# Sine by polynomial on GpSimd, weight splits in order of use, and the first recurrence of a two-layer kernel two steps later

## What is computed

```python
nu = jax.nn.softplus(nu_log); mag = jnp.exp(-jnp.exp(nu)); theta = jnp.exp(theta_log)
A_re = mag * jnp.cos(theta);  A_im = mag * jnp.sin(theta)
gamma = jnp.sqrt(jnp.clip(1.0 - mag * mag, 0.0))
# Bu = x @ (gamma * B).T ; h_t = A * h_{t-1} + Bu_t (complex) ; 32 states
y = einsum(H_re, C_re) - einsum(H_im, C_im) + D * x
h = jax.nn.gelu(einsum('lne,he->lnh', x, proj1) + proj1_bias, approximate=False)
out = einsum('lnh,eh->lne', h, proj2) + proj2_bias
```

## Time and profile before

| | |
|---|---|
| median of the runs | 805.11 us (804.58 to 806.72) |
| the profiled execution, its own time | 806.05 us |
| its span from first to last instruction | 804.2 us |
| PE busy in the span | 783.7 us (97%) |
| DVE, ACT, POOL busy | 699.9, 524.0, 468.4 us |

### The profile page before, as it was taken

The page is one execution under the profiler, slowest core; times in us unless marked ns, Lnnn a source line. Parts: engine busy times, 40 slices in busy tenths (PEclk is TensorE's granted clock), DMA queues, the critical chain, the costliest instruction groups (busy, mean ns, idle before and its releaser), DMA issues.

```text
span 804.2 us, 23023 instructions
## 1 busy us (share of the span) xinstructions
PE 783.7 (97%) x7912; PEld 717.5 (89%) x7912; DVE 699.9 (87%) x2647; ACT 524.0 (65%) x1612; POOL 468.4 (58%) x1245
## 2 busy tenths in 40 slices
PE   7999999999999999999999999999999999999978
PEld 5988999888888889899989999999899998999957
DVE  6798787877787899999898999989999899998885
ACT  4554454445563787777767777777777767777672
POOL 6833022022333776866768677686676867759653
PEclk9999999999999999999999999999999999999999
DMA  8600011000001322232222322222232223312220
GB/s 304 236 22 19 1 66 67 1 1 1 2 6 36 55 45 45 50 53 51 53 39 44 56 55 53 37 47 48 54 61 35 47 43 57 64 34 49 42 41 29
DMA packets 101333, 41.15 MB, mean 51 GB/s; under 512 B 91744, under 2 KB 98400, under 8 KB 100576
## 3 DMA queue, kind: packets, MB, share of 16 engines
q1 hardware_dynamic: 98896, 38.89, 21.7%
q10 hardware_dynamic: 2320, 0.79, 0.4%
HBM read 14.47 MB, written 4.19 MB: 23 GB/s over the span
## 4 chain that ended last, share of the span: by engine, by line
PE 85%; DVE 5%; POOL 3%; issue 2%; SPq 2%; ACT 1%; DMA 1%; ACTq 1%; POOLq 0%; DVEq 0%
PE bank L513 58%; PE bank L719 11%; PE bank L741 8%; PE bank L712 3%; PE bank L577 1%; SPq L478 1%; POOL par L1796 1%; DVE QA L1527 1%; PE bank L587 1%; PE bank L627 1%; PE bank L530 1%; DMA QT<-QA 1%; DVE SM L1556 1%; ACTq L409 1%; DVE PT L1578 1%
## 5 line engine op out<-in xcount | busy, mean ns | idle before, releaser
L1010 ACT ACTIVATE SM<-SM,stb 128x32 f32<-128x32 f32 (+7 forms) x512 | 206.1, 404 | 64.2 <-DVE stb L1556 60.6
L1957 POOL TENSOR_SCALAR SM<-SM,stb 128x32 f32<-128x32 f32 (+7 forms) x512 | 196.0, 404 | 77.6 <-DVE stb L1563 76.1
L513 PE MATMUL bank<-yh,wq_lo 128*128 128x256 f32 x512 | 150.7, 294 | 0.2 <-DVE QA L1527 0.2
L513 PE MATMUL bank<-yh,wq_hi 128*128 128x256 f32 x512 | 144.7, 283 | 0.0
L513 PE MATMUL bank<-yl,wq_hi 128*128 128x256 f32 x512 | 144.7, 283 | 0.0
L719 PE MATMUL bank<-KT,QT 128*128 128x192 f32 (+4 forms) x640 | 121.1, 328 | 3.1 <-DVE stb L1556 3.1
L1556 DVE CUSTOM_DVE_ANT_0 SM<-bank,CONST 128x224 f32<-128x224 f32 (+3 forms) x320 | 97.1, 347 | 21.6 <-PE bank L719 18.7
L719 PEld LDWEIGHTS bank<-KT,QT 128*128 128x128 f32 x640 | 97.5, 190 | 6.8 <-DVE stb L1556 5.2
L1578 DVE STREAM_TRANSPOSE PT<-SM 128x128 f32<-128x128 f32 (+2 forms) x232 | 99.4, 460 | 2.7 <-PE bank L741 2.7
L513 PEld LDWEIGHTS bank<-yh,wq_lo 128*128 128x128 f32 x512 | 97.1, 190 | 1.8 <-DVE QA L1527 0.4
L513 PEld LDWEIGHTS bank<-yh,wq_hi 128*128 128x128 f32 x512 | 97.1, 190 | 0.0
(11 more groups left out here) (215 smaller groups left out, 2081.8 us busy)
## 6 DMA issues: line engine op xcount, KB each, us to landing
QT<-QA SPq DMA_DIRECT2D x248, 64.0 KB, 2.1
PT<-KV SPq DMA_DIRECT2D x256, 16.0 KB, 1.8
out<-fo SPq DMA_DIRECT2D x32, 128.0 KB, 2.0
X<-in_x SPq DMA_DIRECT2D x7, 512.0 KB, 11.0
stage<-in_wqn SPq DMA_DIRECT2D x2, 1024.0 KB, 9.8
stage<-in_wo SPq DMA_DIRECT2D x2, 1024.0 KB, 5.0
stage<-in_w1t SPq DMA_DIRECT2D x4, 256.0 KB, 5.6
stage<-in_w2t SPq DMA_DIRECT2D x2, 512.0 KB, 7.0
```

Of the source, the lines that this page charges most:

```text
L513: i = e.matmul(dst, a, b, start=(first and j == 0), stop=(last and j == 2), skip_group_check=skip)
L1010: i = e.activation(M[:, at], M[:, at], ACT.Exp, bias=S[:, 0, j:j + 1], scale=-1.0, accum_out=S[:, 1, j:j + 1])
L1957: i = e.tensor_scalar(P[:, at], P[:, at], S[:, 2, j:j + 1], 1.0, ALU.mult, ALU.mult)
```

## The change

Parts, as the diff has them:

- **Sine.** ACT's `angles` and the semaphores `ang` and `sin` are gone; the first ACT instruction is now a Gelu, so there is one table load at the start and none before the first gelu. POOL evaluates sine and cosine of the half angles by a polynomial on 128x16, 128x48 and 128x32 tiles: 15 instructions where 10 stood, and 14 small memsets at the start.
- **Splits in order of use.** `w1_high`/`w1_low` of blocks 1, 2, 3 go from step 0 to steps 0, 2, 4; `w2` blocks to steps 1, 3, 5, 6; `b_high` 3 to 5, `b_low` 4 to 6. `l0_norm(1)` starts in step 2 on DVE, not 0. PE's first up product has an order of its own (`l0_first`): the products with the high part of x come first.
- **First turn and first recurrence.** `l0_turn(1, 0)` goes from step 4 to 5, `l0_bu(0)` from 5 to 7. The scan is cut into `rotate` (up to the scan) and `states` (the products `Z`): `rotate(0)` in step 10, `states(0)` in step 11 (both were in 9). Chunk 1's scan goes from 12 to 14 with `l0_bu(1)`, the others stay. `l0_y` of chunk 0 goes from 10, 11 to 12, 13, of chunk 1 from 14, 16 to 16, 17.
- **Magnitude in small pieces.** From step 5 three pieces a step at the step's end, not seven from step 4 ahead of `h_low`.
- **Tables.** POOL writes `tci` and `tsi` ahead of `RR`; `rotate` waits for two of the three, `l0_y` for all.

```diff
+TURN_FIRST = (5, 12, 20, 28, 36, 44, 52)
+BU_AT = (7, 14, 20, 28, 36, 44, 52, 60)
+ROTATE_AT, SCAN_AT = 10, (11, 14, 20, 28, 36, 44, 52, 60)
+Y_AT = ((12, 16, 22, 30, 38, 46, 54, 62), (13, 17, 23, 31, 39, 47, 55, 63))
...
+            def l0_first():
+                sl = slice(0, 128)
+                w.wait_ge("w1h", 1)
+                w.wait_ge("w1l", 1)
+                for k in range(2):
+                    w.wait_ge("xth", k + 1)
+                    e.matmul(fbank[0][:, :], w1l[:, k, sl], xh[0][:, k, :], start=(k == 0), stop=False)
+                    e.matmul(fbank[0][:, :], w1h[:, k, sl], xh[0][:, k, :], start=False, stop=False)
+                for k in range(2):
+                    w.wait_ge("xtl", k + 1)
+                    i = e.matmul(fbank[0][:, :], w1h[:, k, sl], xl[0][:, k, :], start=False, stop=(k == 1))
+                i.then_inc(SEM["f1"], 1)
...
-            def angles():
-                w.wait_ge("ang", 1)
-                w.wait_ge("sin", 1)
-                e.activation(col(48, 16), col(32, 16), ACT.Sin).then_inc(SEM["sin"], 1)
...
-            e.activation(col(56), tsn[:, 0:1], ACT.Sin).then_inc(SEM["sin"], 1)
+            e.activation(trig[:, 15, 0:1], tsn[:, 0:1], ACT.Gelu)
...
-            def scan(c):
+            def rotate(c):
                 w.wait_ge("bu", c + 1)
-                w.wait_ge("tab", 3)
+                w.wait_ge("tab", 2)
...
+            def states(c):
                 took("rot")
                 for b in range(2):
...
+                if g in (0, 2, 4):
+                    w1_low(1 + g // 2)
+                if g == ROTATE_AT:
                     go(make)
-                    scan(c)
+                    rotate(0)
+                if g in SCAN_AT:
+                    c = SCAN_AT.index(g)
+                    if c:
+                        rotate(c)
+                    states(c)
...
-                if g == 0:
+                if g == 2:
                     norm = l0_norm(1)
-                go(norm, 4)
+                go(norm, {2: 1, 3: 4}.get(g, 9))
...
-                if g == 4:
-                    make = magnitude()
-                go(make, 7)
                 if g < 8 * NC:
                     h_low(g)
...
+                if g == 5:
+                    make = magnitude()
+                go(make, 3)
...
+            ts(ab, r8, 0.5, None, ALU.mult)
+            both = ab.unsqueeze(1).broadcast_to([128, 2, 8])
+            tt(q1.rearrange("p (i n) -> p i n", i=2), both, both, ALU.mult)
+            tt(SUMS[:, 0:3, :], ODD, q1.unsqueeze(1).broadcast_to([128, 3, 16]), ALU.mult)
+            tt(q2, q1, q1, ALU.mult, free=True)
+            tt(SUMS[:, 0:3, :], SUMS[:, 0:3, :], EVEN, ALU.add)
...
-            e.tensor_scalar(RR[:, :], RR[:, :], sgnc, 1.0, ALU.mult, ALU.mult).then_inc(SEM["tab"], 1)
             w.wait_ge("mag", 1)
             e.tensor_scalar(tci[:, :], tc[:, :], col(6), 1.0, ALU.mult, ALU.mult).then_inc(SEM["tab"], 1)
             e.tensor_scalar(tsi[:, :], tsn[:, :], col(6), sgn, ALU.mult, ALU.mult).then_inc(SEM["tab"], 1)
+            e.tensor_scalar(RR[:, :], RR[:, :], sgnc, 1.0, ALU.mult, ALU.mult).then_inc(SEM["tab"], 1)
```

More of the change, by code:

```diff
@@ L69 @@
     "tx", "f1", "f2", "bu", "y", "wn_t", "wo_t", "ty", "mi_t", "tk", "tm", "q", "lo", "s", "pv", "o",
-    "w1h", "w2h", "bh", "xth", "gelu", "hsh", "sin", "th0", "wrh", "wnh", "wmh", "lbh", "woh",
+    "w1h", "w2h", "bh", "xth", "gelu", "hsh", "th0", "wrh", "wnh", "wmh", "lbh", "woh",
     "yth", "mi", "kt", "qn", "gx", "mt", "th1", "p", "oth",
@@ L76 @@
     "st", "mx", "r", "qa", "pt", "otl", "ob",
-    "clean", "par", "ang", "nu", "tab", "rt", "fill", "rl", "lr", "kr", "kvr", "n", "qq", "nw", "rs", "oc", "kwk", "kwv",
+    "clean", "par", "nu", "tab", "rt", "fill", "rl", "lr", "kr", "kvr", "n", "qq", "nw", "rs", "oc", "kwk", "kwv",
 )
@@ L573, in l0_y @@
             def l0_y(c, b):
+                w.wait_ge("tab", 3)
                 w.wait_ge("zz", 2 * c + b + 1)
@@ L780, in _ @@
                     l1_tk(0, wbank)
-                if g < 8 * NC:
+                if g == 0:
+                    l0_first()
+                elif g < 8 * NC:
                     l0_up(g // 8, g % 8)
[L783 to L788, removed]
+                if g in BU_AT:
+                    l0_bu(BU_AT.index(g))
+                if g in Y_AT[0]:
+                    l0_y(Y_AT[0].index(g), 0)
                 if g == 21:
@@ L807, in _ @@
                     l0_turn(c + 1, 1)
-                c, r = divmod(g - 4, 8)
-                if r == 0 and 0 <= c < NC - 1:
+                if g in TURN_FIRST:
+                    c = TURN_FIRST.index(g)
                     l0_turn(c + 1, 0)
@@ L816, in _ @@
                     l1_q(0, 3)
-                if g in (11, 16, 23, 31, 39, 47, 55, 63):
-                    c = (11, 16, 23, 31, 39, 47, 55, 63).index(g)
-                    l0_y(c, 1)
+                if g in Y_AT[1]:
+                    l0_y(Y_AT[1].index(g), 1)
             free_shared("ty", 1)
@@ L1837, in _ @@
             done[0] += 1
+            ODD, EVEN, SUMS, PAIRS = (trig[:, i:i + n, :] for i, n in ((0, 3), (3, 3), (6, 4), (10, 2)))
+            q1, q2, q4 = (trig[:, i, :] for i in (12, 13, 14))
+            for k in range(7):
+                at = SUMS[:, 3, :] if k == 6 else (ODD if k % 2 else EVEN)[:, k // 2, :]
+                e.memset(at[:, 0:8], float((-1) ** k / math.factorial(2 * k + 1)))
+                i = e.memset(at[:, 8:16], float((-1) ** k / math.factorial(2 * k)))
+            i.then_inc(SEM["par"], 1)
+            done[0] += 1
             w.wait_ge("nuth", 16)
```

85 lines of the change are left out of this document (29 added, 56 removed).

## The result

The changed kernel has a median of 811.62 us (809.97 to 812.03, 6 executions) against 805.47 us of the kernel before on the same chip (804.58 to 807.30, 6): a ratio on record of 1.0059, 95% interval 1.0044 to 1.0075 (the two medians alone give 1.0076). That is slower by more than 0.3%, and above the range of 802.0 to 810.2. The profiled execution took 811.47 us, its span is 809.7 against 804.2.

The account below looks back on a forecast made before the run. PE was taken to bound from 80 us on, DVE between 40 and 60. A 5.2 us gain, then a 5.5 us stop with low clock, put l0_up(18) 2.3 us later: 805.1 + 2.3 = 807.4 us, range 802.0 to 810.2.

Parts of the forecast that it names:

- ACT freed, +5.2 us at first: At the start: first gelu waits for neither POOL nor a table, so PE gains 5.2 us by the end of l0_down(7).
- The polynomial: nothing, with 1 us to spare: POOL's five extra instructions, 1.4 to 2.0 us, end CS between 39.2 and 41.2, hidden behind the magnitude wait: no cost.
- The magnitude in pieces puts a wait on POOL: POOL's tci waits for DVE's last magnitude piece, in step 9, until 42.1 us; tables and roots queue behind, to 45.1.
- Roots and stop: l0_roots(2) takes 5.1 us on POOL, to 50.2; DVE waits 2.8 before l0_normed(2), PE 5.5 before l0_y(0, 0).
- an estimate of 4.7 us: l0_roots(2) on POOL by the port-sharing rule: all but some four instructions at 0.28 us, sum 0.4 us lower than 5.1.
- Up(18) at 77.3: Start of l0_up(18) on PE: 77.3 us against 74.98 before, +2.3 us, after the long stop and low clock.
- a microsecond that PE gains or loses before that therefore stays to the end: PE is busy without a break from 80 us on, so the shift at l0_up(18), +2.3 us, is the total's.
- rival (c): PE's stops after the restart keep the clock at 0.50 for 6 us more: 3.0 us on top, 810.4 us; chance 0.15.
- The 3.0 us of low clock at the start: After PE's 2.98 us stop up to 17.51, clock 0.50 for 6 us, half of them lost; counted as gained.
- I add the difference to the median: At the sum: the span difference of +2.3 us is added to the runs' median, 805.1 + 2.3 = 807.4 us.
- (a): Clock stays up through PE's stop before l0_y(0, 0): l0_up(18) at 75.1, total 805.2 us; chance 0.15.
- (b): POOL's roots do not bind: rl comes by 47 and not 50, PE stops 2.0 us, total 801.7 us; chance 0.15.

Follow-up runs that it names:

- Experiment 2: Changed kernel with four magnitude pieces a step instead of three, the last in step 8: 810.78 us, ratio 1.0063.
- Experiment 6: Changed kernel with the root of chunk 2 computed on DVE in steps 9 and 10 and l0_roots(2) gone from POOL: 807.60 us, ratio 1.0025.
- experiment 1: Kernel before with the sine part alone (polynomial on POOL, one Gelu table load on ACT), nothing moved: 806.71 us, ratio 1.0018.
- experiment 12: Changed kernel unaltered, run again as the third set of executions: 809.22 us, ratio 1.0048.
- experiment 5: Changed kernel unaltered, run again as the second set of executions: 809.03 us, ratio 1.0056.
- experiment 10: Kernel before with only the rotary weights moved, from step 11 to steps 20 and 22: 805.51 us, ratio 0.9999.
- experiment 8: Changed kernel with the sine back on ACT and POOL's old post-processing, all moves kept: 816.75 us, ratio 1.0139.
- experiment 11: Changed kernel with only the rotary weights moved, as in experiment 10: 810.78 us, ratio 1.0065.
- experiment 7: Changed kernel with chunk 2's root on DVE, states(0) right behind rotate(0), chunk 2's turn in step 13, rotary weights in step 18: 808.13 us, ratio 1.0038.
- experiment 9: As experiment 7, but rope_high in step 20 and rope_low at the end of step 22: 804.69 us, ratio 1.0004.

## Why the prediction was wrong

- **ACT freed, +5.2 us at first: right.** In front of the long stop PE is 5.1 us ahead of the kernel before (the matmul at 40.17 us there starts at 35.03). The two small stops are 0.18 and 0.94 us (0.3 and 1.1 forecast). The trace has its first gelu right behind PE's product, so no table or drain is in the way.
- **"The polynomial: nothing, with 1 us to spare": wrong in its bound, without consequence.** `CS` ended at 41.44, just over the upper bound of 41.2. The cover, the magnitude wait, was only 0.95 us long. Experiment 2 shows that with the cover gone POOL's chain takes its place: `l0_y(0, 0)` starts only 0.13 us earlier.
- **"The magnitude in pieces puts a wait on POOL": right in place, wrong in weight.** `mag` came at 42.2 (42.1 forecast), and removing the wait won 0.13 us (experiment 2).
- **Roots and stop: right in kind, 0.7 us short.** The roots began at 45.53 (45.1) and took 5.33 (5.1); DVE waited 2.97 us (2.8), PE 6.02 (5.5), `l0_y` came at 53.18 (52.5 for `Z`). Experiment 6 confirms the roots as the largest term. The sum of the roots came out near by luck. I took half of the fifteen at 0.40 us and half at 0.28; three took 0.61 to 0.64 each, start to start (46.18 to 48.07), and the others 0.27 to 0.33. The three ended at 46.73, 47.38 and 47.98; the three DVE instructions beside them, all with both sources in SBUF, ended at 46.74, 47.33 and 47.92. Beside `rotate`'s products, with a source in PSUM (43.77 to 45.55), no POOL instruction on 128x32 or 128x4 took more than 0.24. With that the trace agrees with the rule of the Trainium skill (GPSIMD Engine Reference, "1. Specifications"), which names DVE instructions with two SBUF inputs as those that POOL contends with. By that rule I had worked out an estimate of 4.7 us; it falls short because it has 0.40 and not 0.63 for a roots instruction that is held up. `tci` fits in: it took 0.48 us with DVE idle (experiment 1), 0.75 with one such DVE instruction beside it for 0.4 us, and 1.54 with two of them (experiment 2).
- **Up(18) at 77.3: nearly right.** It came at 77.81, so the sum was +2.8 and not +2.3 us; in the third set it came at 78.55.
- **The step that failed is the one that carried the sum to the end:** "a microsecond that PE gains or loses before that therefore stays to the end". It rests on "From 80 us on PE is busy without a break", which was read from the one stretch of 80 to 100 us: the kernel before has stops of 1.18 us before 260.93 and 2.29 before 769.40. In the first profile another 2.5 us were lost at the same two places, 1.7 of them near 264 us and 0.8 near 774, by spells of low clock in untouched code, so that the 3.0 us of up(18) became 5.5. Such spells are not the change's own: experiment 5 has none, and experiment 10, without the change, has one. I had priced a second spell as rival (c) with 0.15, placed it right behind the restart, and cut the range at 810.2 inside that case. The three sets show such spells in 7 of 19 executions; in the first set five of six had them. Their share is larger in that set than in the others; no run here says why, nor whether the change makes them more frequent.
- **The base was one execution too.** The 3.0 us of low clock at the start were taken from a profile in which the clock fell. Experiment 10, with the same stop, kept it up, and PE was 1.9 us ahead by it, not 3.0, in part because it then waited 0.47 us for the low part of `w2`. "I add the difference to the median" assumes that all executions have the same spells. Of the kernel before, 31 of 78 have a mean clock of 0.998 or more; of the changed kernel, whose long stop lowered the clock in all three profiles, none of 19 has. At equal clock (0.996) the median spans are 804.1 before (9 executions) and 807.3 after (12), 3.2 apart, but the medians over all executions are 4.1 apart.
- **The rivals.** (a), the clock stays up through the stop, did not occur: it fell in all six profiles with a stop near 6 us (the changed kernel and experiments 2, 5, 8, 11 and 12). (b), POOL does not bind, was false of this change; experiments 7 and 9 built it, and up(18) then came 2 us early.

The fall of the clock follows no single length of stop: it fell at 1.14 us in experiment 1 (mean 0.76 over 10 to 17 us) and not at the same 1.14 us in the kernel before; at 2.98 us in the kernel before and not at 2.99 in experiment 10; not at 1.73 in experiment 9; and at 4.09 us and more in all nine profiles that have such a stop.

## What to carry over

Taking an engine's stall away only pays if what PE needs next is ready as well: here POOL made both the sine and, later, tables and roots, and the gain reappeared as a longer stop on the chain behind it. Read where the producer's own list ends before moving its consumers. When a change is worth a few us on a kernel that runs PE near full, do not carry one profile's spells of low clock into the sum: compare several executions at equal mean clock, and let the range hold one spell more and one spell less, wherever it falls.

## What was not expected

- An unchanged kernel's mean clock varies from 0.991 to 1.000 between executions and its time from 803.68 to 808.89 us (78 executions); that is wider than most of the effects studied here.
- The same POOL instruction on 128x256 (`tci`) took 0.48 us in experiment 1, 0.75 in the changed kernel and 1.54 in experiment 2, by what DVE did beside it. What experiment 2 won on the wait it gave back there.
- The change was slower by 3 to 6 us, but no arrangement of its parts that was tried was measurably faster than the kernel before; the best, experiment 9, is level with it.
